# Two graph layers over a 256 MB adjacency: column 2 of rows 10 to 15 is taken by seven products in its rows, and rows 0 and 1 are read again as whole rows of 512 nodes

## The reference

```
def _L0_gnn_ref(x, adj, u):
    keep = (u >= 0.1).astype(x.dtype)
    return jnp.matmul(adj, x * keep / 0.9)
def _L1_gnn_ref(input, adj, W, b):
    return adj @ (input @ W) + b
h = jnp.maximum(_layernorm(x, axis=-1), 0.0)
x = x + _L0_gnn_ref(h, adj, u)
h = jnp.maximum(_layernorm(x, axis=-1), 0.0)
x = x + _L1_gnn_ref(h, adj, W, b)
```

## Time and profile before

| | us |
|---|---|
| median of 3 runs (lowest, highest) | 890.52 (890.24, 890.54) |
| time of the profiled execution | 890.25 |
| its span | 888.4 |
| TensorE busy | 868.6 |
| VectorE busy | 560.2 |
| moved by DMA | 363.79 MB |

### The profile page before, as it was taken

How to read it: one execution, slowest core, us unless ns; L and a number is a source line. 1 busy time by engine, 2 the same in 40 slices (tenths; PEclk the granted TensorE clock), 3 DMA queues, 4 the chain that set the end, 5 groups by cost and what they waited for, 6 DMA issues and landing times.

```text
span 888.4 us, 14438 instructions
## 1 busy us (share of the span) xinstructions
PE 868.6 (98%) x5972; PEld 584.4 (66%) x5972; DVE 560.2 (63%) x1207; ACT 45.1 (5%) x132; POOL 1.4 (0%) x11
## 2 busy tenths in 40 slices
PE   5999999999999999999999999999999999999998
PEld 5654567665667554464668666787878778878753
DVE  5655334123153657667677676878778898788724
ACT  3000000000000000000000000000000000000000
POOL 0000000000000000000000000000000000000000
PEclk9899999999999999999999999999999999999999
DMA  9999999999999999999999999999999999999993
GB/s 376 419 419 421 420 421 421 420 421 422 420 421 421 421 421 421 417 421 420 413 420 417 420 418 417 414 417 406 418 412 412 396 410 417 420 421 416 416 417 142
DMA packets 56146, 363.79 MB, mean 409 GB/s; under 512 B 6033, under 2 KB 6289, under 8 KB 15505
## 3 DMA queue, kind: packets, MB, share of 16 engines
q1 hardware_dynamic: 55920, 362.83, 99.1%
q10 hardware_dynamic: 160, 0.03, 0.0%
HBM read 360.74 MB, written 2.10 MB: 408 GB/s over the span
## 4 chain that ended last, share of the span: by engine, by line
PE 81%; DMA 15%; DVE 3%; issue 1%; ACT 0%; SPq 0%; DVEq 0%; ACTq 0%
PE banks L837 32%; PE banks L854 19%; DMA blocks<-in_adj 14%; PE row_sums L810 11%; PE banks L831 7%; PE row_sums L860 6%; PE row_sums L818 6%; DMA x<-in_x 1%; DVE acc L591 0%; DVE mixed L582 0%; PE banks L960 0%; PE banks L927 0%; PE row_sums L927 0%; PE banks L981 0%; DVE quarters L673 0%
## 5 line engine op out<-in xcount | busy, mean ns | idle before, releaser
L837 PE MATMUL banks<-blocks,features 128*64 128x512 f32 (+2 forms) x1720 | 356.4, 506 | 4.8 <-DMA blocks<-in_adj 4.8
L837 PEld LDWEIGHTS banks<-blocks,features 128*64 128x64 f32 x1720 | 180.3, 137 | 117.9 <-issue 70.3
L810 PE MATMUL row_sums<-blocks,features 128*64 128x512 f32 x856 | 216.1, 593 | 0.6 <-DMA blocks<-in_adj 0.6
L711 DVE TENSOR_TENSOR acc<-acc,banks 128x512 f32<-128x512 f32 (+1 forms) x106 | 72.7, 686 | 171.4 <-PE banks L837 157.0
L854 PE MATMUL banks<-quarters,mixed 128*64 128x256 f32 x664 | 157.6, 379 | 0.1
L810 PEld LDWEIGHTS row_sums<-blocks,features 128*64 128x64 f32 x856 | 99.5, 137 | 76.3 <-issue 36.3
L854 PEld LDWEIGHTS banks<-quarters,mixed 128*64 128x64 f32 x664 | 90.5, 137 | 18.1 <-DVE quarters L679 0.6
L831 PE MATMUL banks<-blocks,features 128*64 128x512 f32 x280 | 90.0, 592 | 0.3 <-DVE features L645 0.3
L854 PE MATMUL banks<-quarters,features 128*64 128x256 f32 x332 | 85.3, 379 | 0.0
L860 PE MATMUL row_sums<-blocks,mixed 128*64 128x256 f32 x332 | 85.3, 379 | 0.0
L854 PE MATMUL banks<-blocks,features 128*64 128x256 f32 x332 | 85.2, 379 | 0.0
(11 more groups left out here) (62 smaller groups left out, 537.9 us busy)
## 6 DMA issues: line engine op xcount, KB each, us to landing
blocks<-in_adj SPq DMA_DIRECT2D x256, 1024.0 KB, 15.9
blocks<-in_left SPq DMA_DIRECT2D x42, 1024.0 KB, 25.4
blocks<-in_top SPq DMA_DIRECT2D x27, 1024.0 KB, 25.5
blocks<-in_left SPq DMA_DIRECT2D x26, 512.0 KB, 14.9
x<-in_x SPq DMA_DIRECT2D x2, 1024.0 KB, 7.0
acc<-in_u SPq DMA_DIRECT2D x2, 1024.0 KB, 9.1
out<-x SPq DMA_DIRECT2D x7, 256.0 KB, 2.6
blocks<-in_top SPq DMA_DIRECT2D x2, 768.0 KB, 25.2
```

The costliest lines, as they stand in the source:

```text
L711: nc.vector.tensor_tensor(mine, mine, banks[at, q.bank, :], ALU.add).then_inc(sum_added, 1)
L810: return nc.tensor.matmul(row_sums[at, t.unit % 2, nodes], features[:, tile_of(k, j), 0:D], tile, start=start, stop=last and t.n == unit_l ...
L837: done = nc.tensor.matmul(banks[at, t.sum.bank, nodes], features[:, tile_of(t.k, j), D:2 * D], tile, start=t.n == t.sum.first and j == t.t ...
```

## The change

- In `ORDER`, the items a10.2, a11.2, a12.2, a13.2, a14.2 and a15.2, which stood between o3.13 and o4.13, are gone. In their place s10.2, s11.2, s12.2, s13.2, s14.2 and s15.2 stand in their own rows, each just before the seven of column 3. h0 stands first instead of fourth. All else keeps its place.
- `adj` in DRAM now holds all 16 x 16 blocks. Every reload is one transfer of 8 KB per partition.
- So a reloaded block of rows 0 and 1 lies in SBUF as all others do, and is multiplied in products of 512 nodes. `multiply_last` loses its case for pieces.

```diff
-h4 h8 h12 h0 i4 i8 t0 t1 t2 ...
+h0 h4 h8 h12 i4 i8 t0 t1 t2 ...
-m2.6 b3.2 p0.2 o3.13 a10.2 o3.14 a11.2 o3.15 a12.2 o3.5 o3.4 o3.3 o4.8 a13.2 o4.9 o4.10 a14.2 o4.11 o4.12 a15.2
-o4.13 s4.3 ...
+m2.6 b3.2 p0.2 o3.13 o3.14 o3.15 o3.5 o3.4 o3.3 o4.8 o4.9 o4.10 o4.11 o4.12 o4.13 s4.3 ...
...
-        self.transfers = 2 if kind == "again" and i == 0 else 1
...
-                elif i == 0:
-                    at, n = 2 * P * TILES, GROUP[0][0]
-                    to = blocks[:, slot, 0:at].rearrange("p (h c) -> p h c", h=2)
-                    of = left_0[0:AT[0][2]].rearrange("(h a) p (b c) -> a b p h c", h=2, b=n)[k // n, k % n]
-                    sp.dma_start(to, of).then_inc(block_arrived[slot], 16)
-                    n = GROUP[0][2]
-                    to, of = blocks[:, slot, at:], left_0[AT[0][2] + k // n, :, k % n * at:(k % n + 1) * at]
-                elif i == 1:
-                    n = GROUP[1][0]
-                    to = blocks[:, slot, :].rearrange("p (h c) -> p h c", h=2)
-                    of = left_1.rearrange("(h a) p (b c) -> a b p h c", h=2, b=n)[k // n, k % n]
                 else:
-                    n = len(SPLIT)
-                    to, of = blocks[:, slot, :], adj[(i - n) * (BLOCKS - n) + k - n, :, :]
+                    to, of = blocks[:, slot, :], adj[i * BLOCKS + k, :, :]
...
-                if i >= len(SPLIT):
+                if loads[0].kind != "left":
                     return [(slice(0, BLK), blocks[:, loads[0].slot, j * BLK:(j + 1) * BLK])]
...
-    blocks = np.ascontiguousarray(blocks[len(SPLIT):, len(SPLIT):]).reshape(-1, P, TILES * BLK)
+    blocks = np.ascontiguousarray(blocks).reshape(BLOCKS * BLOCKS, P, TILES * BLK)
```

More of the change, by code:

```diff
@@ L37 @@
 ORDER = """
-h4 h8 h12 h0 i4 i8 t0 t1 t2 t3 t4 t5 i12 i0 t6 t7 j14 j12 u0 u1 u2 u3 j10 j8 j6 u4 j4 j2 u5 j0 u6 u7 k4 v0 v1 v2
+h0 h4 h8 h12 i4 i8 t0 t1 t2 t3 t4 t5 i12 i0 t6 t7 j14 j12 u0 u1 u2 u3 j10 j8 j6 u4 j4 j2 u5 j0 u6 u7 k4 v0 v1 v2
 v3 k6 k8 v4 k10 k12 k14 k2 k0 v5 v6 v7 m0.4 w1 l6 w2 l8 w3 l10 w4 l12 l14 w5 l2 l0 w6 w7 o2.6 p0.1 x1 o2.7 o2.8
 x2 o2.9 o2.10 x3 o2.11 o2.12 x4 o2.13 o2.14 x5 o2.15 o2.5 x6 o2.4 o2.3 x7 o2.2 o3.7 o3.8 o3.9 o3.10 o3.11 o3.12
-m2.6 b3.2 p0.2 o3.13 a10.2 o3.14 a11.2 o3.15 a12.2 o3.5 o3.4 o3.3 o4.8 a13.2 o4.9 o4.10 a14.2 o4.11 o4.12 a15.2
@@ L42 @@
[L42 to L50, removed]
+m2.6 b3.2 p0.2 o3.13 o3.14 o3.15 o3.5 o3.4 o3.3 o4.8 o4.9 o4.10 o4.11 o4.12 o4.13 s4.3 p2.3 p0.3 o4.14 s4.2
@@ new lines @@
+o4.15 o4.7 o4.6 o4.5 o4.4 o5.9 o5.10 o5.11 o5.12 o5.13 o5.14 m4.8 s5.4 p2.4 s5.2 o5.15 s5.3 o5.7 o5.6 o5.5 o6.10
+o6.11 o6.12 o6.13 o6.14 o6.15 s6.5 p4.5 p2.5 s6.2 s6.3 o6.9 s6.4 o6.8 o6.7 o6.6 o7.11 o7.12 o7.13 o7.14 r0.5
+m6.10 s7.6 p4.6 s7.2 s7.3 o7.15 s7.4 o7.9 s7.5 o7.8 o7.7 o8.12 o8.13 o8.14 o8.15 r2.6 s8.7 p6.7 p4.7 s8.2 s8.3
+s8.4 o8.11 s8.5 o8.10 s8.6 o8.9 o8.8 o9.13 o9.14 r0.6 r0.4 o9.15 o9.11 m8.12 s9.8 s9.2 p6.8 s9.3 s9.4 s9.5 s9.6
+r2.7 o9.10 s9.7 o9.9 o10.14 r0.7 o10.15 o10.13 r4.8 s10.9 p8.9 s10.2 s10.3 p6.9 s10.4 s10.5 o10.12 s10.6 s10.7
@@ L51 @@
+o10.11 s10.8 r2.8 o10.10 o11.15 r0.8 o11.13 r4.9 m10.14 s11.10 s11.2 s11.3 p8.10 s11.4 s11.5 s11.6 o11.12 r2.9
+s11.7 s11.8 s11.9 o11.11 r0.9 o12.15 r6.10 o12.14 r4.10 s12.11 s12.2 s12.3 p10.11 s12.4 p8.11 s12.5 s12.6 s12.7
+o12.13 r2.10 s12.8 s12.9 s12.10 o12.12 r0.10 r6.11 o13.14 r4.11 r2.11 m12.15 s13.2 s13.3 s13.12 s13.4 p10.12
+s13.5 s13.6 s13.7 s13.8 s13.9 o13.13 s13.10 s13.11 r0.11 r8.12 o14.15 r6.12 r4.12 s14.13 s14.2 s14.3 p12.13
 s14.4 s14.5 p10.13 s14.6 s14.7 s14.8 s14.9 r2.12 s14.10 o14.14 s14.11 s14.12 r0.12 r8.13 r6.13 r4.13 m14.15
-s15.3 s15.4 b15.14 s15.5 s15.6 p12.14 s15.7 s15.8 s15.9 s15.10 r2.13 s15.11 s15.12 s15.13 r0.13 r10.14 r8.14
@@ L53 @@
-r6.14 r4.14 r2.14 r0.14 p14.15 p12.15 r10.15 r8.15 r6.15 r4.15 r2.15 r0.15
+s15.2 s15.3 s15.4 b15.14 s15.5 s15.6 p12.14 s15.7 s15.8 s15.9 s15.10 r2.13 s15.11 s15.12 s15.13 r0.13 r10.14
+r8.14 r6.14 r4.14 r2.14 r0.14 p14.15 p12.15 r10.15 r8.15 r6.15 r4.15 r2.15 r0.15
 """
@@ L197, in plan @@
         assert free[load.slot] < min(later.first for later in loads[n:]), "a block needs a slot that is still held"
-        count[load.slot] += load.transfers
+        count[load.slot] += 1
         load.before, load.arrived = holder[load.slot], 16 * count[load.slot]
@@ L793, in pieces @@
                     wide = len(tiles) * P
[L794 to L797, removed]
+                    at = (k % GROUP[i][part] * TILES + j) * wide
                     nodes = slice(tiles.start * P, tiles.stop * P)
-                    found.append((nodes, blocks[:, load.slot, at:at + wide]))
+                    found.append((nodes, blocks[:, loads[part].slot, at:at + wide]))
                 return found
@@ L954, in multiply_last @@
                     for half in range(2):
[L955 to L963, removed]
+                        (_, tile), = pieces(last.operands[half], last.k, j)
+                        done = nc.tensor.matmul(banks[half * D:(half + 1) * D, last_bank(part), nodes_of(part)],
+                                                features[:, tile_of(last.k, j), D:2 * D], tile[:, nodes_of(part)],
+                                                start=j == 0, stop=j == TILES - 1)
                 done.then_inc(last_summed, 1)
```

## The result

| | before | changed |
|---|---|---|
| median of 20 runs (lowest, highest), us | 890.32 (889.97, 890.54) | 891.76 (891.59, 892.25) |
| time of the profiled execution, us | 890.25 | 891.88 |
| its span, us | 888.4 | 890.1 |
| TensorE busy, us | 868.6 | 868.5 |
| VectorE busy, us | 560.2 | 572.3 |

The ratio of the changed kernel to the one before is 1.0017, with a 95% interval of 1.001 to 1.0023. So it is slower, by 1.4 us, and less than the 0.2% that the prediction took as its bound, though the interval reaches to 0.23%. The forecast was 892.3, with 890.2 to 894.6 as range. Of its three outcomes the prediction held "slower by over 0.2%" the likelier (0.52); what came is the second, "within" (0.40).

The account below looks back on a forecast made before the run. Loads set the time up to r4.8 at 507.37 us, TensorE's work behind it. 890.25 - 14.9 - 0.7 + 18.1 - 1.4 + 0.7 = 892.05, with the median 0.27 above the profiled execution 892.3 us, range 890.2 to 894.6.

Parts of the forecast that it names:

- six loads ahead of r4.8: Blocks (10..15, 2) leave the load-bound stretch, 2.49 us each, so r4.8's second block lands earlier: -14.9 us.
- reloads ahead of r4.8: Eight blocks of r0.5, r0.6, r0.4 and r0.7 load faster in whole rows: -0.7 us, ends 0.3 to 1.2.
- six sevens: Six sevens enter the stretch behind r4.8, costing TensorE 3.02 us each: +18.1 us.
- pieces behind r4.8: Seven reload pairs, r0.8 to r0.14, lose their pieces and save 0.2 us each: -1.4 us, ends 0.8 and 2.0.
- VectorE: Rows of sevens lengthen and VectorE comes late, mainly for s14.3 in row 14: +0.7 us, ends 0 and 3.1.
- h0 first: In the start-up, h0 saves up to 1.75 us, which the load wait at 217.80 takes back: 0.
- The wait before o4.13: TensorE's longest new wait for a load, in the first stretch, since s4.3's load stands ahead: 3.3 us.
- rival B: Rows 10 to 15: VectorE sets the pace, all six sevens lose 0.51 us, 894.7 us; chance 0.11.
- Rival C: New waits before o4.13 make TensorE's clock fall; one fall is paid from waits, three give 895.5 us; chance 0.06.
- a granted clock of 0.5 behind o4.13: Sign named as showing the forecast wrong: TensorE at half clock behind o4.13, pointing to Rival C.
- A: Whole kernel: TensorE is the bound throughout, so the change is faster, 884.1 us; chance 0.08 with anything like it.
- D: Load order: the change doesn't do what it says, a slot held longer might delay loads, slower; chance 0.03.

Follow-up runs that it names:

- experiment 1: The kernel before with only the six column-2 items moved (a10.2 to a15.2 become s10.2 to s15.2), reloads and h0 as before: 894.00 us, ratio 1.0041.
- experiment 3: The kernel before with a10.2 to a15.2 left out and nothing in their place, so six blocks of the sum are missing: 875.37 us, ratio 0.9831.
- experiment 2: The kernel before in its own order, with only the reloads of rows 0 and 1 in whole rows: 888.43 us, ratio 0.9980.
- experiment 4: The changed kernel with h0 back in fourth place: 891.69 us beside 891.76 for the changed kernel.
- experiment 6: The kernel before with only three items moved (a13.2 to a15.2 become s13.2 to s15.2), reloads and h0 as before: 892.32 us, ratio 1.0023.
- experiment 5: The changed kernel with s14.2 moved from before s14.3 to behind the pair p12.13: 891.23 us, ratio 1.0012 to the kernel before.
- experiment 8: The kernel of experiment 2 with s10.3 to s15.3 turned into ahead items a10.3 to a15.3: 885.98 us, ratio 0.9951 to the kernel before.

## Why the prediction was right

The right-hand column is the ledger of the profiled execution of the changed kernel.

| term | predicted | measured |
|---|---|---|
| six loads ahead of r4.8 | -14.9 | -14.8 (experiment 1), -14.9 (experiment 3); from m2.6 on -15.0 and -14.9 |
| reloads ahead of r4.8 | -0.7 | -1.2 (r4.8 at 492.56 and 491.37), -0.5 in experiment 2; from m2.6 on -1.0 and -0.8 |
| six sevens | +18.1 | +18.1 (3.02 each, but for the waits for VectorE) |
| pieces behind r4.8 | -1.4 | -1.3 |
| VectorE | +0.7 | +0.8 (row 14 0.7, row 12 0.1) |
| h0 first | 0 | 0.0 (experiment 4) |
| sum of the profiled executions | +1.8 | +1.6 (span +1.7) |

**Two stretches and a border.** This carried the forecast and was the right reading of the earlier trace rows. Experiment 3 shows it without the rest: 20.6 us of TensorE's work removed, 14.9 us gained. The same border predicts the sign of the change without any sum: a block costs 2.49 us ahead of it and 3.02 behind it.

**The wait before o4.13** was worked out as 3.3 us and is 3.04, and the row is the one named. The smaller waits ahead of it (0.54 before o4.11 and 0.55 before o4.12) are there too.

**Reloads ahead of r4.8.** The term was taken from a loss in GB/s read in a single window. By r4.8's start alone its size seems to depend on the run: 0.5 us in experiment 2, 1.2 in the changed kernel against experiment 1. Part of this spread is older than the reloads. At m2.6, over 130 us before the first block of a reload is needed, the executions already differ by up to 0.3 us. Counted from m2.6's start, eight kernels give this:

| kernel | reloads | column-2 blocks moved | m2.6 | r4.8 | between | without the moved loads |
|---|---|---|---|---|---|---|
| before | pieces | 0 | 217.80 | 507.37 | 289.57 | 274.6 |
| experiment 6 | pieces | 3 | 217.97 | 500.12 | 282.15 | 274.7 |
| experiment 1 | pieces | 6 | 218.00 | 492.56 | 274.56 | 274.6 |
| experiment 3 | pieces | 6 (left out) | 217.82 | 492.45 | 274.63 | 274.6 |
| experiment 2 | whole | 0 | 218.07 | 506.87 | 288.80 | 273.9 |
| experiment 4 | whole | 6 | 217.76 | 491.18 | 273.42 | 273.4 |
| experiment 5 | whole | 6 | 218.04 | 491.50 | 273.46 | 273.5 |
| changed | whole | 6 | 217.79 | 491.37 | 273.58 | 273.6 |

The last column takes 2.49 us off for each of the six blocks that is still loaded ahead of r4.8. The four kernels with pieces lie within 0.1 us of each other, the four with whole rows 0.7 to 1.3 us lower, 1.0 on the average. So the term was mis-sized by 0.3 us in its middle, and the price of pieces is about 0.13 us for a block of 2.49. Why experiment 2 gains less than the other three stays open. By the Trainium skill ("DMA: Bandwidth & Descriptors", Specifications: line rate from 512 B on) the term would be 0. All four kernels with whole rows speak against that, by 5% of a load. A block of row 0 with pieces came in two transfers besides; these runs don't separate the size of the pieces from the number of transfers.

**Pieces behind r4.8.** The pairs of row 0 take 3.43 us, on the chain of the changed kernel first r0.8, then r0.11 with r8.12:

```profile
536.37 3.43 PE banks L821 x16
...
701.34 6.87 PE banks L821 x32
```

Before they were 3.49 and 7.17, the first of them cut at its edges. All seven together are seen in experiment 2: the stretch behind r4.8 is 1.1 us shorter although s14.3 waits 0.2 us that it didn't before, so the seven gain 1.3 us, 0.19 each where 0.2 was taken.

**VectorE.** The place (s14.3, then row 12), the mechanism (two sevens in a row where the pair p12.13 stands behind them) and the size were right, 0.4 and 0.6 us of waits in two weight loads, of s14.2 and of s14.3, in place of one wait of 0.6. By the starts of the sevens these cost TensorE 0.3 and 0.4 us, and a third in row 12 costs 0.1. Experiment 5 confirms it: with the pair between them 0.5 us come back. The far end, 0.51 us for each of six sevens (rival B, 894.7), didn't happen, and no wait for the quarters of a seven stands in rows 10, 11 and 15; the prediction's reason for that, a pair that follows and gives the lead back, is what experiment 5 shows for row 14 alone.

**The clock.** Rival C's first step came true and its end didn't. Behind the 3.04 us of idleness before o4.13 the granted clock fell, once. The windows of the changed kernel around it (the clock is the third number from the right):

```profile
250.00:254.00 4.00, 1.53 (x6) 0.48 (x8) 2.56 (x4) 0.00 (x0) 0.00 (x0) 0.94 1.02 424
254.00:258.00 4.00, 4.00 (x24) 2.16 (x22) 0.00 (x0) 0.00 (x0) 0.00 (x0) 0.63 1.02 420
258.00:262.00 4.00, 4.00 (x28) 1.64 (x25) 0.00 (x0) 0.00 (x0) 0.00 (x0) 1.00 1.02 420
...
254.00:256.00 2.00, 2.00 (x10) 0.94 (x8) 0.00 (x0) 0.00 (x0) 0.00 (x0) 0.50 0.99 414
```

A mean of 0.94 over 4 us is 2 x 0.06 x 4 = 0.5 us at half clock (1.2 of 2.4 GHz), one of 0.63 is 3.0 us: 3.4 us together, in which TensorE did 1.7 us less work, half of the 3.4 us that the prediction priced. As the prediction had it for one fall, it was paid from the waits behind it (m4.8 took 1.6 us longer than its products before, 0.3 now), and r4.8 started where the loads put it. A second fall did not come; no other wait in this stretch is longer than 1.5 us. The prediction had named "a granted clock of 0.5 behind o4.13" as a sign that it was wrong. That sign came (0.50 from 254 to 256 us) and the forecast held, so the sign was badly chosen: only a fall that its waits can't pay would have spoken against it. That the idle state is the slow one, as the Trainium skill has it ("TensorE: Matmul & The Clock Gate", The HAM clock gate), agrees with the place: the fall stands behind the longest idle time after the start-up.

**The other rivals.** A (884.1) falls with experiment 3. D is excluded by r4.8's landing at 491.24, 16.0 us sooner, near the 15.6 forecast.

**The rest of 0.56 us between 892.32 and 891.76.** 0.17 of it lies in the terms (892.05 forecast, 891.88 profiled): the reload term was 0.5 too small against the starts of r4.8, and three others were off by 0.1 each the other way. The larger part, 0.39, is the step from the profiled execution to the median, taken as +0.27 and measured as -0.12. It says nothing on the mechanism.

## What to carry over

When two resources are both near 100% busy, look for the last wait of the one for the other: it cuts the run into a stretch in which a piece of work costs what its load takes and a stretch in which it costs what its products take, and in this kernel moving work across the cut was worth the difference of the two, and beyond that only what it did to the waits for VectorE. The direction that pays follows at once (here towards the early stretch, against what the change did), and so does its limit: the idle time ahead of the cut, less the waits for a third engine that the idle time has hidden. Work saved by a faster form in the load-bound stretch turns into waiting, so the same saving must be counted by its place.

## What was not expected of the hardware

**One wait, one fall.** In the profiled executions of the five kernels with twelve "one" items in a row between o3.13 and o4.13 and a wait of 3.0 us before o4.13 (the changed kernel and experiments 1, 3, 4 and 5) the granted clock fell once, at the end of this wait or right behind it, for 3.4 us. In experiment 6, with a wait of 2.16 us at the same place and three "ahead" items left ahead of it, it did not; its windows there:

```profile
258.00:262.00 4.00, 1.90 (x10) 0.76 (x12) 2.25 (x4) 0.00 (x0) 0.00 (x0) 1.00 1.01 422
262.00:266.00 4.00, 4.00 (x36) 2.32 (x34) 0.00 (x0) 0.00 (x0) 0.00 (x0) 1.00 1.02 420
```

One product at either clock, from s4.3 on TensorE's timeline of the changed kernel, of the same shape:

```profile
254.94 0.63 PE L838 MATMUL banks<-blocks,features 128*64 128x256 f32 x1
...
257.22 0.38 PE L838 MATMUL banks<-quarters,mixed 128*64 128x256 f32 x1
```

Whether the length of that one wait decides or the smaller waits ahead of it count too, these runs don't separate. Nor does the fall come in every execution. The mean clock over the changed kernel's whole execution is 0.994 in the profiled one and in five others of the 20, and 1.00 in three. The three took 891.67, 891.85 and 892.25 us, the six 891.65 to 892.00. So the fall cost 1.7 us of TensorE's work and nothing of the kernel's time, as is to be expected in a stretch that waits for loads. In the other stretch it should cost 1.7 us; no run shows that.

**Two near-full resources.** In experiment 8 TensorE is busy 321.07 of 322 us while the 16 DMA engines move 421 GB/s. No sign shows that one slows the other: a seven that waits for nothing takes 3.02 us, and the loads move no faster to speak of where TensorE idles (424 GB/s from 250 to 254 us of the changed kernel, with TensorE busy 1.53 of 4 us).
